# Stages in new places, layer norm outputs on GpSimd, an uneven max pass, and two head groups in one bank of sums

## The chip, the cores and the metric

The kernel runs on one core of a Trainium2 chip (trn2). The core's engines are TensorE (PE; its weight loads are PEld), VectorE (DVE), ScalarE (ACT), GpSimd (POOL) and SyncE (SP), which issues most of the DMAs. The metric is the device time of one execution in microseconds. Inputs and outputs are float32.

## The reference

One transformer block with post layer norm and no learned scale, on 16 sequences of 512 tokens and 128 features: causal attention with 16 heads of 8 features, in which the heads 0, 1 and 2 weigh one third of the keys each 1.6 times and are normalised again, and a feed-forward part of three dense layers whose weights are +1 or -1.

```python
def attention(x):                                  # (16, 512, 128)
    q, k, v = split(x @ c_attn_w + c_attn_b, 3)    # 16 heads of 8
    scores = where(causal, q @ k.T / sqrt(8), finfo.min)
    attn = softmax(scores)
    scaled = attn * mult[None, :, None, :]         # 1.6 in one region of keys, heads 0, 1, 2
    scaled = scaled / sum(scaled, -1)
    attn = where(head in (0, 1, 2), scaled, attn)
    return (attn @ v) @ c_proj_w + c_proj_b
def ffn(x):                                        # k0 (256, 512), k1 (512, 512), k2 (512, 128)
    h = relu(s0 * (concat([x, -x]) @ where(k0, 1, -1))) * 2
    h = relu(s1 * (h @ where(k1, 1, -1))) * 2
    return s2 * (h @ where(k2, 1, -1))
x = layernorm(x + attention(x))
x = layernorm(x + ffn(x))
```

## The kernel before

The program is a software pipeline over the 16 batches, written out engine by engine. `iteration(n)`, for n from -2 to 17, has G = 4 groups of four heads and STEPS = 10 steps in each; a step is written (g, t). In one iteration each engine works on several batches: the attention of batch n, the max pass of batch n + 1, q, k and the stacks of batch n + 2, the end of the attention and the first layer norm of batch n - 1, the feed-forward part of n - 1 and n - 2.

In each step TensorE computes one bank of scores for the max pass (`max_scores`, L825, into one of three banks `max_ps`) and one bank of the real, transposed scores (`scores`, L849, into one of two banks `score_ps`). VectorE takes masked row maxima from the first (`take_max`, L643), ScalarE exponentiates the second (`exp`, L516), and GpSimd sets the masked part of the result to 0 (`mask`, L423), three times in a group. Steps 0 to 3 hold the 512 keys of one head each, steps 4 to 7 pieces of 384 and 128, steps 8 and 9 two of 256. At t = 1, 3, 5, 7 TensorE adds the exponentials of the group before, times v and a column of ones (`sums`, L882), into the one bank `av_ps`, four heads at 32 rows each; at t = 9 ScalarE copies it to `avT` (`sums_out`, L523).

Queries and keys are split in three bfloat16 parts, which DMAs on SP's queue stack to 72 rows (`stack_half`, L310), so that one matmul gives the float32 score; three more rows subtract the row maximum. The maxima are split in three parts on VectorE (`split_rowmax`), transposed on TensorE (stages rowmax0 and rowmax1, L893), copied on VectorE (L683) and put into the stack by a DMA on ScalarE's queue (`rowmax_rows`, L542). Feed-forward activations are split in a high and a low part (h_hi and h_lo, L430 and L432 on GpSimd; x_hi and x_lo, L727 and L732, on VectorE).

All other work goes through two banks `bank_ps`, which the stages take in turn. The table PLACES gives for each stage the batch it works on, relative to n, the step at which TensorE fills the bank, and the step at which ScalarE or VectorE empties it; the order of the table is the order of the banks. Each engine runs its own list of instructions in order and waits on counting semaphores for the others. GpSimd's order is written out by hand in its `iteration`. So a stage that is late holds all that stands behind it on its engine. The stages: xT (transposes of the input), q, k, v, tok_0 to tok_3 (transposes of avT by 128 tokens; VectorE then normalises: reciprocal L703, product L705), attnT and proj (L967), x1T (transposes of the first layer norm's output, the sources named res), ffn0_m and ffn1_m (L909, L910), ffn2T (L924, L925) and ffn2 (its transposes).

A layer norm is: statistics (L712), aggregation (L718), minus mean and variance plus epsilon (L721, L722) on VectorE, `rstd_of` on GpSimd (a power and a product, L437 and L440), and four outputs of 128 tokens (`layernorm_out`, L534) on ScalarE.

## Time and profile before

| | |
|---|---|
| median of 3 runs | 1007.99 us (995.96, 1007.99, 1011.67) |
| the profiled execution | 994.16 us, its span 992.4 us |
| mean granted TensorE clock | 0.928 of full speed |
| PE busy | 864.0 us, 87% |
| PEld, DVE busy | 439.0 and 671.9 us |
| ACT, POOL busy | 605.0 and 502.6 us |
| first real scores, last | 73.6 us, 935.5 us |

The span is the time from the first to the last instruction of one profiled execution. The engines work side by side, so their busy times add to more than it. Between the start and the end of the program the iterations repeat with a constant period, which is what matters here.

### The profile page before, as it was taken

What the parts mean: (1) busy time and instruction counts of PE and PEld (TensorE: products, weight loads), DVE (VectorE), ACT (ScalarE), POOL (GpSimd) and SP (SyncE); (2) the same over time, 40 slices, a digit from 0 to 9 for tenths busy, and PEclk for the clock granted to TensorE, in tenths of its full rate; (3) what the DMA queues carried; (4) which work ended last, traced back from release to release, by engine and by line L of the source; (5) the groups of instructions that cost most, each with busy time, mean ns of one, the idle gap of its engine ahead of it and who ended that gap; (6) DMA issues with size and microseconds to landing.
All of it is one profiled execution on the core that took longest, in us unless ns stands there. A gap on an engine that the chain in (4) does not pass through costs nothing.

```text
span 992.4 us, 17320 instructions
## 1 busy us (share of the span) xinstructions
PE 864.0 (87%) x5824; PEld 439.0 (44%) x5824; DVE 671.9 (68%) x2784; ACT 605.0 (61%) x1106; POOL 502.6 (51%) x625
## 2 busy tenths in 40 slices
PE   2349698999999899989999998989999898999866
PEld 1114244545454454545454453545455454535343
DVE  3367578575867768595967669595857769694234
ACT  2106467566766667576757667576756767576733
POOL 1103145637564654647574664646565655547540
PEclk8558899979999997999999799999989999999887
DMA  3653635345453534455443435455443425300000
GB/s 77 68 76 60 71 51 69 45 71 56 52 63 46 74 45 66 53 71 60 53 63 45 66 45 75 49 71 59 57 54 50 70 34 73 38 23 2 23 11 11
DMA packets 66142, 53.19 MB, mean 54 GB/s; under 512 B 4518, under 2 KB 64006, under 8 KB 66054
## 3 DMA queue, kind: packets, MB, share of 16 engines
q1 hardware_dynamic: 65190, 51.30, 40.2%
q8 instruction: 47, 0.77, 0.4%
q10 hardware_dynamic: 864, 0.79, 0.3%
q14 instruction: 41, 0.34, 0.2%
HBM read 9.24 MB, written 4.19 MB: 14 GB/s over the span
## 4 chain that ended last, share of the span: by engine, by line
PE 51%; DVE 23%; POOL 9%; ACT 5%; DMA 5%; issue 4%; SPq 2%; ACTq 1%; POOLq 0%; DVEq 0%
PE av_ps L882 10%; DVE max_ps L643 10%; PE max_ps L825 10%; PE score_ps L849 8%; PE bank_ps L909 5%; POOL h_lo L432 5%; PE bank_ps L910 5%; PE bank_ps L808 4%; PE bank_ps L955 3%; DMA stack<-rowmaxT 3%; DVE stats L712 3%; POOL h_hi L430 2%; DMA stack<-parts 2%; DVE rowmax L643 2%; PE bank_ps L944 2%
## 5 line engine op out<-in xcount | busy, mean ns | idle before, releaser
L643 DVE CUSTOM_DVE_ANT_0 max_ps<-max_ps,future 128x512 f32<-128x512 f32 (+3 forms) x1024 | 480.3, 514 | 232.7 <-PE max_ps L825 229.6
L516 ACT ACTIVATE e<-score_ps 128x512 f32<-128x512 f32 x640 | 365.1, 595 | 187.7 <-PE score_ps L849 184.5
L825 PE MATMUL max_ps<-stack 72*128 72x512 bf16 (+3 forms) x1024 | 260.5, 318 | 59.9 <-DVE rowmax L643 36.1
L849 PE MATMUL score_ps<-stack 75*128 75x512 bf16 (+3 forms) x1024 | 253.8, 310 | 20.8 <-DMA stack<-rowmaxT 16.1
L423 POOL TENSOR_SCALAR_AFFINE_SELECT e<-e 128x512 f32<-128x512 f32 x256 | 160.2, 646 | 129.7 <-ACT e L516 129.7
L882 PE MATMUL av_ps<-e,vaug 128*9 128x512 f32 (+3 forms) x2048 | 194.3, 453 | 3.1 <-ACT avT L523 1.7
L825 PEld LDWEIGHTS max_ps<-stack 72*128 72x128 bf16 x1024 | 83.5, 101 | 218.0 <-DVE rowmax L643 98.3
L432 POOL TENSOR_TENSOR h_lo<-full,h_hi 128x512 fp32r<-128x512 f32 x120 | 153.4, 1278 | 10.0
L508 ACT ACTIVATE full<-bank_ps,scales 128x512 f32<-128x512 f32 x128 | 86.8, 687 | 114.3 <-PE bank_ps L910 93.1
L643 DVE DVE_READ_ACCUMULATOR2_ANT rowmax<- 128x1 f32 x1024 | 143.2, 140 | 0.0
L849 PEld LDWEIGHTS score_ps<-stack 75*128 75x128 bf16 x1024 | 90.1, 100 | 78.7 <-issue 23.8
L437 POOL TENSOR_TENSOR rstd<-var_eps,minus_half 128x4 f32<-128x4 f32 x32 | 32.5, 1015 | 151.0 <-DVE var_eps L722 151.0
L909 PE MATMUL bank_ps<-h_hi,w 128*128 128x512 f32 x256 | 106.5, 416 | 2.0 <-POOL h_lo L432 1.7
L430 POOL CAST h_hi<-full 128x512 fp32r<-128x512 f32 x120 | 73.0, 609 | 65.0 <-ACT full L508 65.0
L910 PE MATMUL bank_ps<-h_lo,w 128*128 128x512 f32 x256 | 101.1, 395 | 0.0
L406 POOL TENSOR_TENSOR qk<-qk,parts 128x1024 f32<-128x1024 f32 x15 | 31.9, 2127 | 122.5 <-ACT qk L508 122.5
L882 PEld LDWEIGHTS av_ps<-e,vaug 128*9 128x9 f32 x2048 | 31.2, 88 | 86.4 <-issue 79.7
L534 ACT ACTIVATE res<-res,shift,rstd 128x128 f32<-128x128 f32 x128 | 52.5, 483 | 15.0 <-POOL shift L440 15.0
L909 PEld LDWEIGHTS bank_ps<-h_hi,w 128*128 128x128 f32 x256 | 48.3, 189 | 20.8 <-POOL h_lo L432 6.1
L910 PEld LDWEIGHTS bank_ps<-h_lo,w 128*128 128x128 f32 x256 | 48.5, 189 | 8.7
L808 PE MATMUL bank_ps<-ident,avT 128*128 128x128 f32 x256 | 40.2, 280 | 3.3 <-ACT qk L508 2.6
L955 PE MATMUL bank_ps<-xT,wqk 128*128 128x512 f32 x64 | 38.6, 690 | 2.1 <-ACT xT L508 0.8
(83 smaller groups left out, 791.6 us busy)
## 6 DMA issues: line engine op xcount, KB each, us to landing
stack<-parts SPq DMA_DIRECT2D x288, 128.0 KB
x_in<-in_L_attn_hidden_states SPq DMA_DIRECT2D x16, 256.0 KB, 5.7
x_res<-in_L_attn_hidden_states SPq DMA_DIRECT2D x16, 256.0 KB, 11.4
out_x<-res SPq DMA_DIRECT2D x16, 256.0 KB, 10.9
stack<-rowmaxT ACTq DMA_DIRECT2D x32, 24.0 KB
e<-in_L_ffn_k SPq DMA_DIRECT2D x1, 256.0 KB, 3.5
wc<-in_L_attn_c_attn_w SPq DMA_DIRECT2D x1, 192.0 KB
e<-in_L_ffn_k SPq DMA_DIRECT2D x1, 128.0 KB, 3.3
```

What stands on the lines that cost most here:

```text
L423: last = nc.gpsimd.affine_select(out=ap, in_=ap, compare_op=ALU.is_ge, fill=0.0, base=0, pattern=[[0, 4], [1, P]], channel_multiplier=-1)
L430: nc.gpsimd.tensor_copy(h_hi[layer][:, m, :], full[:, full_slot(b, k), :]).then_inc(hi_ready, 1)
L432: nc.gpsimd.tensor_tensor(h_lo[layer][:, m, :], full[:, full_slot(b, k), :], h_hi[layer][:, m, :].bitcast(F32), ALU.subtract).then_inc(spl ...
L508: nc.scalar.activation(out_ap, bank_ps[:, u[0], :], func, **kw).then_inc(bank_free[u[0]], 1)
L516: nc.scalar.activation(e[g % 2][:, t, :], score_ps[:, t % 2, :], ACT.Exp, scale=SCALE).then_inc(exped, 1)
L643: return nc.vector.tensor_tensor_reduce(out=scored_block, in0=scored_block, in1=future[:, P * (T - 1 - qt):S], scale=1.0, scalar=NEG, op0= ...
L808: last = nc.tensor.transpose(bank[:, P * i:P * i + P], src, ident[:])
L825: return nc.tensor.matmul(out_ap[:, col:col + width], st[0:QK_ROWS, h, 0, P * qt:P * qt + P], st[0:QK_ROWS, h, 1, 0:width], start=True, st ...
L849: return nc.tensor.matmul(out_ap[:, col:col + width], st[0:ALL_ROWS, h, 1, P * kt:P * kt + P], st[0:ALL_ROWS, h, 0, P * kt:S], start=True, ...
L882: last = nc.tensor.matmul(av_ps[32 * j:32 * j + R + 1, P * kt:S], vaug[b.parity][:, kt, G * g + j, :], src, start=(order == 0), stop=(orde ...
L909: nc.tensor.matmul(bank, w, hi, start=(i == 0), stop=False)
L910: last = nc.tensor.matmul(bank, w, lo, start=False, stop=(i == len(pairs) - 1))
```

## The change

- PLACES and the tables beside it put nearly all stages to other steps. ffn1_0 and ffn1_1 now run at the end of the iteration before (group 3), ffn1_2, ffn1_3, q, k and ffn2T in group 0, tok in group 1, x1T and ffn0 from (2,6) to (3,3). xT has two buffers.
- Max pass: at the three steps of MAX_TWICE two banks of max scores are computed and taken, at the three of MAX_NONE none (`max_steps`).
- The groups of heads are now even and odd heads of a half (`head`). v has, for a pair of heads, 9 columns, 16 of zeros, 9 columns; a group takes 25 of these 34. Two groups thus add into different rows of one bank, which is copied once for both (avT has two parts, not four), and tok_0 and tok_1 transpose two blocks of 128 tokens each.
- Layer norm outputs: `normalise_tokens` on GpSimd (L472) takes the place of L534 on ScalarE. Statistics have steps of their own (LN_STATS).
- The high parts of ffn0_2 and ffn0_3 are cast on VectorE, not on GpSimd.
- SP's queue: the store of the output stands behind the load of the residual, which waits for rowmax0's bank.

```diff
 PLACES = (
-    ("ffn1_0", -2, (0, 4), (0, 4)),
+    ("xT", 2, (0, 0), (0, 0)),
+    ("q", 2, (0, 3), (0, 4)),
     ("v", 1, (0, 7), (0, 8)),
-    ("xT", 2, (0, 9), (0, 9)),
-    ("q", 2, (1, 0), (1, 1)),
-    ("tok_0", -1, (1, 2), (1, 2)),
-    ("rowmax1", 0, (1, 4), (1, 4)),
-    ("ffn2", -2, (2, 2), (2, 3)),
-    ("proj", -1, (2, 6), (2, 6)),
-    ("x1T", -1, (3, 2), (3, 2)),
+    ("ffn2", -2, (0, 9), (0, 9)),
+    ("tok_0", -1, (1, 0), (1, 0)),
+    ("rowmax1", 0, (1, 3), (1, 3)),
+    ("proj", -1, (1, 7), (1, 9)),
+    ("x1T", -1, (2, 6), (2, 6)),
+    ("ffn0_0", -1, (2, 8), (2, 8)),
+    ("ffn0_1", -1, (2, 9), (2, 9)),
-    ("ffn0_0", -1, (3, 5), (3, 5)),
-    ("ffn0_1", -1, (3, 5), (3, 5)),
+    ("ffn1_0", -1, (3, 6), (3, 7)),
...
-NEGMAX_SPLIT = (((3, 0), (3, 0), (3, 1), (3, 2)), ((1, 0), (1, 0), (1, 1), (1, 2)))
-
-NEGMAX_ROWS = ((3, 5), (1, 5))
-
-LN_VAR = ((2, 7), (2, 3))
-LN_OUT = (((3, 0), (3, 0), (3, 0), (3, 0)), ((2, 7), (2, 7), (2, 7), (2, 7)))
+FFN2_STEPS = ((0, 5), (0, 5), (0, 6), (0, 6))
+
+HIGH_STEPS = {"x1T": (2, 7), "ffn0_0": (2, 9), "ffn0_1": (3, 0), "ffn0_2": (3, 2), "ffn0_3": (3, 3),
+              "ffn1_0": (3, 7), "ffn1_1": (3, 9), "ffn1_2": (0, 1), "ffn1_3": (0, 4)}
+
+HIGH_ON_POOL = ("ffn0_0", "ffn0_1", "ffn1_0", "ffn1_1", "ffn1_2", "ffn1_3")
+
+MIDDLE_STEP = (0, 8)
+
+NEGMAX_SPLIT = (((3, 0), (3, 0), (3, 1), (3, 2)), ((0, 9), (1, 0), (1, 1), (1, 2)))
+
+NEGMAX_ROWS = ((3, 5), (1, 4))
+
+LN_STATS = ((2, 1), (3, 5))
+LN_VAR = ((2, 2), (3, 6))
+
+MAX_TWICE = ((0, 1), (0, 3), (0, 5))
+MAX_NONE = ((2, 1), (2, 2), (2, 7))
...
+        def max_steps(n, g, t):
+
+            each = [2 if (g_, t_) in MAX_TWICE else 0 if (g_, t_) in MAX_NONE else 1
+                    for g_ in range(G) for t_ in range(STEPS)]
+            first = sum(each[:STEPS * g + t])
+            for i in range(first, first + each[STEPS * g + t]):
+                quarter = i // STEPS
+                b = n + 1 if quarter else n
+                if live(b):
+                    yield b, (quarter + 3) % G, i % STEPS
+
+        def head(g, j):
+
+            return HALF * (g // 2) + 2 * j + g % 2
+
+        highs_of_dve = [w for w in HIGH_STEPS if w not in HIGH_ON_POOL]
+        HIGHS_OF_DVE = len(highs_of_dve)
...
+                if live(n + 1):
+                    wait_free(sp, use_of(n + 1, "rowmax0"))
                 if live(n):
                     if n.c > 0:
                         wait_free(sp, use_of(n + -1, "proj"))
                     sp.dma_start(x_res[:], x_tok[n.times(1)]).then_inc(xres_loaded, 16)
+                if live(n + -2):
+                    store(n + -2)
...
+            def normalise_tokens(b, i):
                 pool.wait_ge(ln_step[i], b.times(4, 3))
                 nc.gpsimd.tensor_tensor(rstd[:, i, :], var_eps[:, i, :], minus_half[:],
                                         ALU.pow).then_inc(rstd_ready[i], 1)
                 pool.wait_ge(rstd_ready[i], b.times(2, 1))
                 nc.gpsimd.tensor_tensor(shift[:, i, :], neg_mean[:, i, :], rstd[:, i, :],
                                         ALU.mult).then_inc(rstd_ready[i], 1)
+                pool.wait_ge(rstd_ready[i], b.times(2, 2))
+                x = res2 if i else res1
+                for t in range(T):
+                    ins = nc.gpsimd.tensor_scalar(x[:, t, :], x[:, t, :], rstd[:, i, t:t + 1], shift[:, i, t:t + 1],
+                                                  ALU.mult, ALU.add)
+                ins.then_inc(ln_step[i], 1)
...
+                low(1, 1)
+                low(1, 2)
+                low(1, 3)
                 masks(0, 0)
-                low(1, 0)
-                low(1, 1)
+                split_qk(0)
                 masks(0, 1)
-                low(1, 2)
+                split_qk(2)
                 masks(0, 2)
                 bias_residual()
-                split_qk(0)
                 masks(1, 0)
-                low(1, 3)
-                split_qk(2)
                 masks(1, 1)
+                layernorm_out(0)
                 masks(1, 2)
-                rstd_of_layer(1)
                 masks(2, 0)
-                rstd_of_layer(0)
-                masks(2, 1)
-                masks(2, 2)
-                masks(3, 0)
                 low(0, 0)
                 low(0, 1)
+                masks(2, 1)
+                low(0, 2)
+                masks(2, 2)
+                low(0, 3)
+                masks(3, 0)
+                layernorm_out(1)
+                low(1, 0)
                 masks(3, 1)
-                low(0, 2)
-                low(0, 3)
                 masks(3, 2)
...
+            def sums_out(b, pair):
+                act.wait_ge(summed, b.times(G, 2 * pair + 2))
+                if pair == 0 and b.c > 0:
+                    wait_full(act, use_of(b + -1, "tok_1"))
+                nc.scalar.activation(avT[:, pair, :], av_ps[:], ACT.Copy).then_inc(av_out, 1)
...
+                src = bank_ps[:, u[0], :].rearrange("p (t h o r) -> p t h o r", t=T, o=2, r=R)
+                bias = bv[:].rearrange("p (h o r) -> p h o r", o=2, r=R)
+                for o in range(2):
+                    last = nc.vector.tensor_tensor(
+                        va[:, :, :, ODD * o:ODD * o + R], src[:, :, :, o, :],
+                        bias[:, :, o, :].unsqueeze(1).broadcast_to([P, T, HALF, R]), ALU.add)
+                last.then_inc(bank_free[u[0]], 1)
...
                         src = e[g % 2][:, 8 + j // 2, 2 * P * (j % 2):2 * P * (j % 2) + 2 * P]
-                    last = nc.tensor.matmul(av_ps[32 * j:32 * j + R + 1, P * kt:S],
-                                            vaug[b.parity][:, kt, G * g + j, :], src,
-                                            start=(order == 0), stop=(order == 3))
+                    vals = vaug[b.parity][:, kt, head(g, j) // 2, (R + 1) * odd:(R + 1) * odd + ODD]
+                    last = nc.tensor.matmul(av_ps[32 * j:32 * j + ODD, P * kt:S], vals, src,
+                                            start=(order == 0 and not odd), stop=(order == 3 and odd == 1))
```

VectorE, before, from the taking of v at (0,8) to the copy of the transposed row maxima (rowmaxT) at (1,5), of one middle iteration; the left-out rows are maxima (`ISA`).

```order
L691 TENSOR_TENSOR vaug<-bank_ps,bv 128x64x8
L695 TENSOR_TENSOR vaug<-vaug,mult 128x4x3x8
L643 ISA max_ps,rowmax<-max_ps,future 128x256
...
L666 CAST rowmax_parts<-rowmax 128x4x8
L668 TENSOR_TENSOR rowmax_rest<-rowmax,rowmax_parts 128x32
...
L670 CAST rowmax_parts<-rowmax_rest 128x4x8
...
L703 RECIPROCAL recip<-bank_ps 128x16
L705 TENSOR_TENSOR attn<-bank_ps,recip 128x128
L672 TENSOR_TENSOR rowmax_parts<-rowmax_rest,rowmax_parts 128x4x8
...
L683 COPY rowmaxT<-bank_ps 24x512
```

The same stretch of VectorE in the changed kernel, up to the last part of the row maxima at (1,2):

```order
L719 TENSOR_TENSOR vaug<-bank_ps,bv 128x32x8 x2
L724 TENSOR_TENSOR vaug<-vaug,mult 128x4x2x8
...
L668 ISA max_ps,rowmax<-max_ps,future 128x512
...
L789 TENSOR_TENSOR res<-bank_ps,res 128x512
L691 CAST rowmax_parts<-rowmax 128x4x8
...
L735 RECIPROCAL recip<-bank_ps 128x32
L737 TENSOR_TENSOR attn<-bank_ps,recip 128x256
L693 TENSOR_TENSOR rowmax_rest<-rowmax,rowmax_parts 128x32
...
L695 CAST rowmax_parts<-rowmax_rest 128x4x8
...
L737 TENSOR_TENSOR attn<-bank_ps,recip 128x256
L697 TENSOR_TENSOR rowmax_parts<-rowmax_rest,rowmax_parts 128x4x8
```

The residual add of the second layer norm (L789) and both takings of attention transposes now stand between v and the last part of the row maxima.

TensorE, before, around the transposes of the first layer norm's output (sources res), from the projection on:

```order
L967 MATMUL bank_ps<-wp,attnT 128x128 x4
...
L882 MATMUL av_ps<-e,vaug 9x256 x4
...
L882 MATMUL av_ps<-e,vaug 9x512 x4
...
L808 MATMUL bank_ps<-ident,res 128x128 x4
...
L882 MATMUL av_ps<-e,vaug 9x384 x4
L893 MATMUL bank_ps<-ident_bf,rowmax_parts 24x128 x4
...
L882 MATMUL av_ps<-e,vaug 9x128 x4
L909 MATMUL bank_ps<-x_hi,w 128x512
L910 MATMUL bank_ps<-x_lo,w 128x512
```

The same place in the changed kernel; the projection now stands nine steps ahead of it:

```order
L921 MATMUL av_ps<-e,vaug 25x128 x4
L862 MATMUL max_ps<-stack 128x384
...
L886 MATMUL score_ps<-stack 128x384
...
L845 MATMUL bank_ps<-ident,res 128x128 x4
...
L921 MATMUL av_ps<-e,vaug 25x256 x4
L862 MATMUL max_ps<-stack 128x256 x2
L886 MATMUL score_ps<-stack 128x256 x2
L948 MATMUL bank_ps<-x_hi,w 128x512
L949 MATMUL bank_ps<-x_lo,w 128x512
```

The transposes moved from (3,2) to (2,6), behind the projection by nine steps and not by six, and ffn0_0 comes two steps behind them; before, it was three, with the row-max transposes between.

GpSimd, before, from the first layer norm's power on:

```order
L437 TENSOR_TENSOR rstd<-var_eps,minus_half 128x4
L440 TENSOR_TENSOR shift<-neg_mean,rstd 128x4
L423 AFFINE_SELECT e<-e 128x4x128 x4
L430 CAST h_hi<-full 128x512
L432 TENSOR_TENSOR h_lo<-full,h_hi 128x512
L430 CAST h_hi<-full 128x512
L432 TENSOR_TENSOR h_lo<-full,h_hi 128x512
L423 AFFINE_SELECT e<-e 128x4x128 x2
```

The same in the changed kernel:

```order
L464 TENSOR_TENSOR rstd<-var_eps,minus_half 128x4
L467 TENSOR_TENSOR shift<-neg_mean,rstd 128x4
L472 TENSOR_SCALAR res<-res,rstd,shift 128x128 x4
L445 AFFINE_SELECT e<-e 128x4x128 x2
L454 CAST h_hi<-full 128x512
L459 TENSOR_TENSOR h_lo<-full,h_hi 128x512
L454 CAST h_hi<-full 128x512
L459 TENSOR_TENSOR h_lo<-full,h_hi 128x512
L445 AFFINE_SELECT e<-e 128x4x128 x2
L459 TENSOR_TENSOR h_lo<-full,h_hi 128x512
L445 AFFINE_SELECT e<-e 128x4x128
```

The four outputs stand behind the power, and only one mask instruction pair lies between them and the split of ffn0_0; the masks of group 2's second set (the second `AFFINE_SELECT` x2 row) now come behind the splits of ffn0_0 and ffn0_1.

## Rows read from the trace of the kernel before

**Rows 1.** Busy time by stretch: us, then PE, PEld, DVE, ACT, POOL, clock, DMA.

```profile
376.17:433.59 57.42, 54.79 (x368) 28.53 (x364) 40.95 (x173) 38.01 (x70) 32.69 (x39) 0.91 0.45 57
433.59:488.52 54.93, 51.21 (x368) 26.43 (x364) 41.10 (x173) 37.40 (x70) 32.17 (x39) 1.00 0.49 59
```

**Rows 2.** Waits from 433.59 to 488.52: us in total, times, longest.

```profile
PEld max_ps L825 <- DVE rowmax L643: 5.7, 9, 1.1
...
PE max_ps L825 <- DVE rowmax L643: 2.2, 3, 1.4
```

**Rows 3.** Timeline from 434 to 440 us, first layer norm: start, duration, engine, line.

```profile
434.31 0.87 DVE L712 BATCH_NORM_STATS2 stats<-res 128x6 f32<-128x128 f32 x4
...
435.81 0.38 DVE L718 BATCH_NORM_AGGREGATE moments<-stats 128x2 f32<-128x6 f32 x4
...
436.10 0.38 PE L825 MATMUL max_ps<-stack 72*128 72x512 bf16 x1 [1.36 <-DVE rowmax L643]
...
436.55 1.01 POOL L437 TENSOR_TENSOR rstd<-var_eps,minus_half 128x4 f32<-128x4 f32 x1 [3.16 <-DVE var_eps L722]
...
437.87 1.65 ACT L534 ACTIVATE res<-res,shift,rstd 128x128 f32<-128x128 f32 x4 [0.54 <-POOL shift L440]
...
439.57 0.66 PE L808 MATMUL bank_ps<-ident,res 128*128 128x128 f32 x4 [0.15 <-ACT res L534]
```

**Rows 4.** Busy time by stretches of 4 us (columns as in rows 1).

```profile
376.00:380.00 4.00, 2.05 (x19) 0.94 (x12) 3.93 (x24) 3.91 (x9) 0.87 (x1) 1.00 0.72 103
...
384.00:388.00 4.00, 4.00 (x25) 1.66 (x28) 2.96 (x10) 1.37 (x4) 1.17 (x1) 0.50 0.57 80
```

**Rows 5.** Timeline from 428 to 433 us, steps (2,2) to (2,5).

```profile
428.53 0.70 DVE L643 CUSTOM_DVE_ANT_0 max_ps<-max_ps,future 128x512 f32<-128x512 f32 x1
...
429.14 0.69 DVE L756 TENSOR_TENSOR res<-bank_ps,res 128x512 f32<-128x512 f32 x1
...
429.40 0.66 PE L808 MATMUL bank_ps<-ident,attn 128*128 128x128 f32 x4
...
429.89 0.38 PE L825 MATMUL max_ps<-stack 72*128 72x384 bf16 x2
...
430.12 0.38 PE L849 MATMUL score_ps<-stack 75*128 75x384 bf16 x2
...
432.06 0.60 DVE L643 CUSTOM_DVE_ANT_0 max_ps<-max_ps,future 128x384 f32<-128x384 f32 x1
...
432.82 0.60 DVE L643 CUSTOM_DVE_ANT_0 max_ps<-max_ps,future 128x384 f32<-128x384 f32 x1
```

**Rows 6.** Groups of instructions, first the page's, then by form: busy, mean ns.

```profile
L423 POOL TENSOR_SCALAR_AFFINE_SELECT e<-e 128x512 f32<-128x512 f32 x256 | 160.2, 646 | 129.7 <-ACT e L516 129.7
L882 PE MATMUL av_ps<-e,vaug 128*9 128x512 f32 (+3 forms) x2048 | 194.3, 453 | 3.1 <-ACT avT L523 1.7
L430 POOL CAST h_hi<-full 128x512 fp32r<-128x512 f32 x120 | 73.0, 609 | 65.0 <-ACT full L508 65.0
L882 PEld LDWEIGHTS av_ps<-e,vaug 128*9 128x9 f32 x2048 | 31.2, 88 | 86.4 <-issue 79.7
L909 PEld LDWEIGHTS bank_ps<-h_hi,w 128*128 128x128 f32 x256 | 48.3, 189 | 20.8 <-POOL h_lo L432 6.1
...
L703 DVE RECIPROCAL recip<-bank_ps 128x16 f32<-128x16 f32 x64 | 16.2, 253 | 32.1 <-PE bank_ps L808 32.0
L691 DVE TENSOR_TENSOR vaug<-bank_ps,bv 128x512 f32<-128x512 f32 x16 | 11.0, 684 | 0.0
L377 POOL TENSOR_SCALAR_AFFINE_SELECT ident<-ident 128x128 f32<-128x128 f32 x1 | 0.3, 292 | 0.2 <-POOL e L373 0.2
```

**Rows 7.** Timeline from 408 to 411 us: a GpSimd and a VectorE instruction side by side.

```profile
408.90 1.29 POOL L432 TENSOR_TENSOR h_lo<-full,h_hi 128x512 fp32r<-128x512 f32 x1
...
409.50 0.81 DVE L695 TENSOR_TENSOR vaug<-vaug,mult 128x96 f32<-128x96 f32 x1
```

**Rows 8.** The chain that ended last, from 105 to 123 us.

```profile
109.72 10.41 DMA stack<-rowmaxT
```

235 lines of the change are left out of this document (113 added, 122 removed).

## The prediction, made blind

> **What bounds the kernel now.** I read first the stretches from one residual add after the projection to the next, which give the length of one period of the steady state: 54.93 us at full clock with TensorE busy 51.21, while VectorE is busy 41.1, ScalarE 37.4 and GpSimd 32.2 [rows 1]. So TensorE sets the pace, but not all of the time. The waits of that period are next: VectorE's maxima hold TensorE's weight loads for 5.7 us and its matmuls for 2.2 us [rows 2]. The two overlap and the busy share counts drains, so what TensorE loses lies between 3.7 us (54.93 - 51.21) and 7.9 us (the sum of the two waits); I take **5.4 us**, which I get when I compare steps of equal work with each other. The timeline shows where: after the projection VectorE runs the residual add, four statistics and four aggregations between its maxima, and TensorE stands for 1.36 us [rows 3]. The transposes of the layer norm output (L808, 439.57) start 3.1 us after the variance (GpSimd's pow, which waits for it, starts at 436.55).
>
> The second thing is the clock. In the period from 376.17 the granted clock was 0.91 on the mean and the period lasted 57.42 us [rows 1]. It fell to 0.50, that is from 2.4 to 1.2 GHz, right behind a stretch in which TensorE was busy 2.05 of 4 us while VectorE and ScalarE were full [rows 4]. It is the same place of the program as in rows 3. It costs 2.5 us (57.42 - 54.93) and comes in one period of three, so 0.83 us per period; the mean period is 55.76 us.
>
> **The change, part by part, for one period at full clock.**
>
> *Transposes of attention.* Two groups of heads now share the bank of sums, so four fills of four transposes become two. A fill holds TensorE for 0.49 us (429.40 to 429.89, [rows 5]): two of them less is **-1.0 us**. Two copies of avT and eight layer norm outputs leave ScalarE: the outputs alone are 8 x 0.41 us (1.65 for four, [rows 3]), but it is not what TensorE waits for, so this is worth nothing by itself. The weights of the sums grow from 9 to 25 columns. A 9-column load takes 88 ns and a 128-column one 189 ns [rows 6], so 16 columns are about 13 ns by these rows; 128 loads a period give 0 (hidden, as loads overlap matmuls) to 1.7 us. I take **+0.3**, near the hidden end, since a period's loads are busy for only 26 of its 55 us [rows 1].
>
> *First pile on VectorE.* TensorE's heavy stages (ffn1, q, k) leave the end of group 0 and the start of group 1. Count from the start of step (0,8) to the second row-max transposes at (1,3). A plain step costs TensorE 0.44 us: two matmuls that start 0.22 apart [rows 5]. The sums of a group take 3.0 us (194.3 / 64, [rows 6]), and by their columns (512 and 384 of 1280, and some overhead) about 1.9 of it lie at t = 1 and 3. TensorE's own work is 6 x 0.44 + 1.9 + 3 fills x 0.45 = 5.9 us. VectorE has five maxima (0.61 us for three of them, from 428.53 to 429.14, and 0.76 for two, from 432.06 to 432.82, [rows 5]), 3.35; the biases of v, two of 0.42 (the 684 ns of L691 less the time of 256 of its 512 columns, [rows 6]) and two small products of 0.2 to 0.8; the residual add 0.69 (429.14, [rows 5]); twice the reciprocal of 32 columns (253 ns for 16, so 0.35) with the product of 256 (as L691, 0.42), 1.6 with what passes between them; and four pieces of the row-max split, 32 columns each, at 0.2. Sum 7.8 us, and it starts 0.4 after TensorE does. That is a wait of 2.3 us at the rowmax transposes. It can be 3.3: the product L695, of only 96 columns, lasted 0.81 us when a GpSimd subtraction was running, ending 0.12 after it [rows 7], and the change puts both of GpSimd's long qk splits just there. I take **2.7**. In the kernel before, this same stretch holds ffn1_3 and the q and k matmuls, and the wait is not seen.
>
> *Layer norm 1.* VectorE's own order then gives: proj ends, residual add, one maximum, statistics 0.87, aggregation and two scalars 0.65. Then GpSimd: pow and shift 1.3 (436.55 to 437.87, [rows 3]), and four outputs of 128x128, which no row shows on GpSimd. Bounds: an affine_select of 128 columns takes 292 ns, a cast of 512 columns 609 ns [rows 6]; so 0.25 to 0.6 each. I take 0.3, near the row of equal width. From the variance to the x1T transposes this is 2.6 us (before: 3.1). TensorE has between them only (2,3) to (2,6) and is ahead by up to three maxima; the two maxima left out there make VectorE's way shorter by 1.4 us. Placed against each other the wait at x1T is 0.9 to 1.5 us, and 2.4 at the upper price: I take **1.2**. Then ScalarE's copy 0.6, VectorE's x_hi and x_lo 1.1 (estimates: passes over 512 columns, each at most the 684 ns of L691) and 0.3 of handing over make 2.0 us against 1.3 us of TensorE's work before ffn0_0: **0.85**.
>
> *GpSimd between group 2 and 3.* Its order is now both parts of ffn0_0, both parts of ffn0_1, and only then the mask of group 2's second set, on which the sums at (3,3) wait. ffn0_1 reaches GpSimd about 2.6 us after its matmuls begin (exponentials, the copy of the sums, and its own 0.7 stand before it on ScalarE); then 0.61 + 1.29 us for the parts and two masks of 0.65 [rows 6, 7]. TensorE needs 4.5 us to get to the same sums: **1.3 us** of waiting. It was not there before, where the masks stood in front.
>
> *The rest.* The cast of ffn0_2 and ffn0_3 on VectorE (below 0.69 each, as L691) lies in group 3, where I count 12.7 us of TensorE work against 11.0 of VectorE: hidden. ffn2T, v, ffn2 and ffn1 find their operands ready by my count; xT, with two buffers, and ffn1_2 at the start of an iteration lose **0.2** for a bank. The store of the output now stands behind the residual's load on SP's queue, which waits for the row-max copy at (3,4); both have a whole group 0, some 15 us of TensorE's work, before the bias add and the second residual add want them. At the start of the program four small memsets more stand before the first transpose, +0.6 us; at the end the layer norm outputs leave ScalarE, two token fills are gone, about -1 us.
>
> **Sum.** 54.93 - 5.4 (old waits) - 1.0 + 0.3 + 2.7 + 1.2 + 0.85 + 1.3 + 0.2 = 55.1 us, so at full clock the period does not change. TensorE's own work falls from 49.5 to 48.5 us and the waits grow from 5.4 to 6.3.
>
> What is left is the clock. The change cuts the long wait after the projection into pieces: none of the waits above leaves TensorE under half busy for as long as in rows 4. I expect fewer falls, and a mean period near 55.1 instead of 55.76: 14 periods x 0.65 = -9 us. Profiled execution 994.16 us, of which the span is 992.4 and 1.8 lie around it; after: **985**. The median of three runs, 1007.99, lies 13.8 us above the profiled one; by rows 1 that is five or six more falls of 2.5 us. With fewer of them in the changed kernel its median should lie close to its best run: I forecast **988 us**.
>
> A page of the Trainium skill speaks against the layer norm outputs on GpSimd: "GPSIMD Engine Reference", section "Performance versus the Vector engine", calls it the wrong choice for ordinary elementwise arithmetic, about twice as slow as VectorE. The rows show what leaves here is not VectorE's work but ScalarE's, at 0.41 us an output [rows 3]; no row has the same output on VectorE, so no row bears the factor out or refutes it. By the rule the outputs would be nearer to my upper price, and the wait at x1T nearer to 2.4 us.
>
> **Rivals.**
>
> *The piles are smaller than I placed them.* VectorE is busy only three quarters of a period [rows 1], and if the maxima of group 0, run early, let it meet group 1 with an empty queue and nothing of GpSimd blocks it, the wait of 2.7 falls to about 1 and those of 1.2 and 1.3 to about 0.5 each. Period 52.6: 14.5 x (55.76 - 52.6) = 46 us less, 948 us. For it: three maxima less where the layer norm is. Against it: VectorE's 7.8 us against TensorE's 5.9 are sums of rows, and no order of them makes them shorter. 0.24.
>
> *Falls as before.* The waits of 2.7 and then 1.2 + 0.85 lie close together, TensorE dips as low as before, and 0.83 us a period stays: 55.9, 994.16 + 2 = 996, median about 1006. The same time comes out if the 25-column loads are not hidden (+1.4), so that the shared bank gives nothing: that is the case in which the change doesn't do what it says. 0.25.
>
> *Slower: TensorE idles in one piece until x1T.* The LN outputs cost 0.6 us each on GpSimd, x1T comes 2.4 us late, ffn0_0 0.85 behind it, and the clock falls in every period, not in one of three: 55.1 + 1.2 + 2.5 = 58.8 against 55.76, so 14.5 x 3.0 = +44 us: 1038 us by the profiled execution. It decides when an output takes more than about 0.45 us. For it: 0.6 is the price of a 512-column instruction [rows 6]. 0.15. A smaller mechanism points the same way: the row-max rows of the second half leave at (1,4), one step earlier, but only some 4 us before the scores at (2,0) want them, and such a transfer took 10.41 us when others were in flight [rows 8]. The stack's transfers should be over by then.
>
> **Numbers.** My forecast has 0.36. The median of 1007.99 puts faster by over 2% below 987.8 and slower above 1028.2; about 2% is what a measurement of this kernel tells from no change, as its runs spread from 996 to 1012. Faster: the first rival whole and half of the forecast, 0.42. Slower: most of the third rival, 0.13. Same: 0.45. The range goes from 948 to 1022, with the tail of the slower case left out.
>
> **What the profile after would show.** Periods of about 55 us with VectorE near 40; a wait of 2 to 3 us of TensorE before the row-max transposes of the second half, on VectorE's split; one of about 1 us before the transposes of the layer norm output, on GpSimd's outputs at about 0.3 us; one of about 1 us before the sums of group 2 on the mask; avT's fills 32 instead of 64; fewer dips of the granted clock. I am wrong if the outputs on GpSimd take 0.45 us or more, if the period is below 53.5 or above 56.5 us at full clock, or if the clock falls in each period.

## The result, and the profile after

The changed kernel takes 1017.91 us, the median of 10 runs (1010.14 to 1035.66), beside 1003.15 us for the kernel before on the same chip: the ratio is 1.0139, with a 95% interval of 1.0095 to 1.0183. Medians are of all runs; ratios and intervals, here and below, leave out the runs that are over 1.5% slower than the fastest of the same kernel. Forecast were 988 us and a gain. It is 1.4% slower. The time lies in the range that was given (948 to 1022); the direction is wrong.

The profiled execution took 1010.14 us, with a span of 1008.4 (992.4 before). The first line of the page, busy time and share by engine:

```profile
PE 841.2 (83%) x5696; PEld 433.7 (43%) x5696; DVE 710.0 (70%) x2788; ACT 536.0 (53%) x946; POOL 542.8 (54%) x722
```

VectorE was busy 671.9 us before and should have lost some; it gained 38. The busy times by stretch (columns as in rows 1), from one batch's first score matmul to the next: one period at full clock, eleven periods together, and two stretches at the start of the second batch.

```profile
351.28:407.35 56.07, 50.06 (x357) 26.43 (x356) 43.44 (x173) 33.27 (x60) 34.76 (x46) 1.00 0.44 58
238.50:858.36 619.86, 557.17 (x3918) 293.87 (x3916) 478.34 (x1893) 366.04 (x650) 382.37 (x496) 0.99 0.44 57
126.75:144.40 17.65, 16.37 (x83) 6.68 (x84) 8.71 (x35) 8.12 (x15) 3.94 (x4) 0.72 0.54 74
144.40:158.05 13.65, 11.99 (x89) 6.03 (x89) 12.41 (x46) 7.62 (x14) 5.81 (x6) 0.87 0.01 4
```

A period at full clock takes 56.07 us, with TensorE busy 50.06. In the kernel before, the same two views give the rows below. Its periods repeat by threes, 54.31, 54.92 and 58.0 us, the last with a fall of the clock; they are not constant. Eleven take 610.99.

```profile
561.70:616.01 54.31, 50.78 (x365) 26.50 (x364) 41.09 (x173) 37.29 (x70) 31.13 (x39) 1.00 0.49 60
227.22:838.21 610.99, 573.76 (x4006) 297.11 (x4005) 451.65 (x1893) 413.16 (x760) 354.49 (x429) 0.97 0.47 58
```

So TensorE's work fell by 0.7 us as reckoned, and its idle time grew from 3.5 (54.31 - 50.78) to 6.0 us. The mean period, clock falls included, went from 55.54 (610.99 / 11) to 56.35 (619.86 / 11). What ended TensorE's waits in the period from 351.28 (waited for, us in total, times, longest; they answer to rows 2):

```profile
PE bank_ps L845 <- ACT avT L556: 1.3, 1, 1.3
PE bank_ps L931 <- DVE rowmax_parts L697: 1.2, 1, 1.2
PE bank_ps L845 <- POOL res L472: 1.1, 1, 1.1
PE av_ps L921 <- POOL e L445: 1.1, 1, 1.1
PE bank_ps L948 <- DVE x_lo L766: 0.7, 1, 0.7
PE bank_ps L948 <- ACT full L541: 0.4, 1, 0.4
```

They are, in the order of the rows: avT's transposes at (1,0), the row-max transposes at (1,3), x1T at (2,6), the sums at (3,3), ffn0_0 at (2,8), the first matmuls of ffn1 at (0,0). The prediction had a wait at all of these places but the first: it put the whole of group 1's wait on VectorE's split at (1,3) and nothing on ScalarE's copy to avT, which stands behind ScalarE's middle part of q and k. The matmuls' waits on VectorE's maxima of rows 2 are gone. The timeline ahead of the second of these waits shows what fills VectorE (start, duration, engine, line; rows 7 had this pattern once):

```profile
370.18 0.69 DVE L668 CUSTOM_DVE_ANT_0 max_ps<-max_ps,future 128x512 f32<-128x512 f32 x1
...
370.38 2.13 POOL L430 TENSOR_TENSOR parts<-qk,parts 128x1024 bf16<-128x1024 f32 x1 [1.82 <-ACT parts L615]
...
370.79 0.69 DVE L789 TENSOR_TENSOR res<-bank_ps,res 128x512 f32<-128x512 f32 x1
371.39 1.16 DVE L691 CAST rowmax_parts<-rowmax 128x32 bf16<-128x32 f32 x1
...
373.07 1.26 POOL L486 TENSOR_TENSOR x_res<-x_res,bp 128x512 f32<-128x512 f32 x1
...
373.80 0.58 DVE L693 TENSOR_TENSOR rowmax_rest<-rowmax,rowmax_parts 128x32 f32<-128x32 f32 x1
```

A cast of 32 columns takes 1.16 us and ends at 372.55, GpSimd's subtraction at 372.51. The next piece of the split ends at 374.38, GpSimd's add at 374.33. The maximum (370.18) and the residual add (370.79), each with one operand in PSUM, take their usual 0.69 beside the same subtraction. Over the whole execution L691 has a mean of 1032 ns, L693 498 and L695 465; in the kernel before the same three had 331, 387 and 185. The layer norm's chain (answers to rows 3):

```profile
386.01 1.02 POOL L464 TENSOR_TENSOR rstd<-var_eps,minus_half 128x4 f32<-128x4 f32 x1 [4.00 <-DVE var_eps L755]
...
387.42 1.74 POOL L472 TENSOR_SCALAR res<-res,rstd,shift 128x128 f32<-128x128 f32 x4
...
389.21 0.66 PE L845 MATMUL bank_ps<-ident,res 128*128 128x128 f32 x4 [1.15 <-POOL res L472]
```

From pow to the transposes it takes 3.2 us; four outputs take 1.74, 0.44 us each. The row-max transfers at the start, from the chain that ended last (answers to rows 8):

```profile
65.25 12.96 DMA stack<-rowmaxT
...
115.51 11.19 DMA stack<-rowmaxT
```

**Where 16 us of span came from.** The first score matmul starts at 78.3 us instead of 73.6 (+4.8). The first two periods take 48.4 and 55.7 us instead of 46.6 and 48.7 (+1.8, +7.0; in the second the clock is at 0.72 for 17.65 us, above). The 13 periods from there take 7.7 us more, and the end after the last batch's first score 5.3 less (95.7 for 101.0).

The 4.8 us are in part of one execution: a second profile of the kernel before (c0 below) has its first score at 75.6.

Below, "full clock" is a period in which the clock did not fall, "mean" that of the same eleven periods, and a step's time runs from its first score matmul to the next step's.

### The profile page after: what moved, and what is told of

It reads as the page before. It is cut to its first block, busy times and chain, and to the rows that moved or that the text cites. A ratio compares the mean times of both kernels' runs of the same rounds, so it can differ in the third digit from the quotient of the medians.

```text
span 1008.4 us, 16988 instructions
## 1 busy us (share of the span) xinstructions
PE 841.2 (83%) x5696; PEld 433.7 (43%) x5696; DVE 710.0 (70%) x2788; ACT 536.0 (53%) x946; POOL 542.8 (54%) x722
## 4 chain that ended last, share of the span: by engine, by line
PE 52%; DVE 19%; POOL 13%; DMA 5%; ACT 4%; issue 4%; SPq 2%; ACTq 0%; POOLq 0%; DVEq 0%
PE av_ps L921 9%; PE max_ps L862 9%; PE score_ps L886 7%; PE bank_ps L948 7%; DVE max_ps L668 7%; PE bank_ps L949 6%; POOL h_lo L459 4%; PE bank_ps L994 3%; POOL res L472 3%; PE bank_ps L845 3%; ACT full L541 3%; DMA stack<-rowmaxT 2%; DMA stack<-parts 2%; POOL h_hi L454 2%; POOL e L445 2%
## 5 line engine op out<-in xcount | busy, mean ns | idle before, releaser
L862 PE MATMUL max_ps<-stack 72*128 72x512 bf16 (+3 forms) x1024 | 249.6, 315 | 26.5 <-DMA stack<-parts 19.4
L886 PE MATMUL score_ps<-stack 75*128 75x512 bf16 (+3 forms) x1024 | 249.3, 306 | 22.8 <-DMA stack<-rowmaxT 18.7
L921 PE MATMUL av_ps<-e,vaug 128*25 128x512 f32 (+3 forms) x2048 | 194.2, 452 | 18.1 <-POOL e L445 17.8
L862 PEld LDWEIGHTS max_ps<-stack 72*128 72x128 bf16 x1024 | 80.0, 100 | 175.1 <-issue 87.9
L886 PEld LDWEIGHTS score_ps<-stack 75*128 75x128 bf16 x1024 | 94.6, 100 | 91.0 <-ACT e L549 25.3
L454 POOL CAST h_hi<-full 128x512 fp32r<-128x512 f32 x90 | 54.9, 610 | 76.5 <-ACT full L541 76.5
L921 PEld LDWEIGHTS av_ps<-e,vaug 128*25 128x25 f32 x2048 | 37.7, 102 | 89.6 <-issue 55.8
L948 PEld LDWEIGHTS bank_ps<-h_hi,w 128*128 128x128 f32 x256 | 48.8, 190 | 22.5 <-ACT full L541 8.3
L472 POOL TENSOR_SCALAR res<-res,rstd,shift 128x128 f32<-128x128 f32 x128 | 56.3, 455 | 3.3
L949 PEld LDWEIGHTS bank_ps<-h_lo,w 128*128 128x128 f32 x256 | 48.8, 191 | 9.0
L430 POOL TENSOR_TENSOR parts<-qk,parts 128x1024 bf16<-128x1024 f32 x15 | 31.9, 2128 | 24.7 <-ACT parts L615 24.7
## 6 DMA issues: line engine op xcount, KB each, us to landing
x_in<-in_L_attn_hidden_states SPq DMA_DIRECT2D x16, 256.0 KB, 16.3
```

Source lines behind the costliest of these rows:

```text
L454: nc.gpsimd.tensor_copy(hi, whole).then_inc(hi_by_pool, 1)
L472: ins = nc.gpsimd.tensor_scalar(x[:, t, :], x[:, t, :], rstd[:, i, t:t + 1], shift[:, i, t:t + 1], ALU.mult, ALU.add)
L862: return nc.tensor.matmul(out_ap[:, col:col + width], st[0:QK_ROWS, h, 0, P * qt:P * qt + P], st[0:QK_ROWS, h, 1, 0:width], start=True, st ...
L886: return nc.tensor.matmul(out_ap[:, col:col + width], st[0:ALL_ROWS, h, 1, P * kt:P * kt + P], st[0:ALL_ROWS, h, 0, P * kt:S], start=True, ...
L921: last = nc.tensor.matmul(av_ps[32 * j:32 * j + ODD, P * kt:S], vals, src, start=(order == 0 and not odd), stop=(order == 3 and odd == 1))
L948: nc.tensor.matmul(bank, w, hi, start=(i == 0), stop=False)
```

## Experiments

### The waits of the changed kernel, one by one

**e1: masks of (2,1) ahead of the low part of ffn0_1** on GpSimd.

```diff
-                low(0, 1)
                 masks(2, 1)
+                low(0, 1)
```

> The changed kernel, with one line moved in GpSimd's list: the masks of group 2's second set (2,1) stand before the split of ffn0_1, not behind it. In the changed kernel TensorE stands about 1.0 us per period before the sums at step (3,3) (2.72 us for a step whose work is 1.7). Theory A (each wait is its own and returns when its cause goes): the period falls from 56.08 to about 55.1 us, the run by about 14 us. Theory B (VectorE is the bound from group 1 to group 3; a wait removed comes back at the next place): the wait of (3,3) goes to the row-max transposes behind it, since VectorE's split and its two casts lie there, and the period stays within 0.3 us of 56.08.

1016.42 us, ratio 1.0124 (1.0027 to 1.0221). The wait for the mask is gone, but step (3,3) only falls from 2.72 to 2.46 us; in its place the row-max transposes there wait 0.7 us for L697 (1.9 us in two waits where there was 1.2 in one). Full clock 55.82, 0.25 less. Theory B.

**e2: ScalarE's middle part of q and k one step later.**

```diff
-MIDDLE_STEP = (0, 8)
+MIDDLE_STEP = (0, 9)
```

> The changed kernel with ScalarE's cast of the middle part of q and k one step later (0,9), so that it no longer stands before the copy of the sums (avT) on which the token transposes at (1,0) wait (1.5 us of waiting there, 1.2 us more at the row-max transposes of (1,3)). If ScalarE's copy is the cause of both, 1 us of the 2.7 goes and the period falls to about 55.1. If VectorE's pile between (0,8) and (1,2) is, as the prediction had it, the wait only moves from (1,0) to (1,3), and the period stays within 0.3 us of 56.08.

1080.17 us in its one run. Step (1,0) falls from 2.39 to 1.44 us, as avT's copy now stands ahead of the middle part, but (1,2) and (1,3) grow from 0.88 and 2.91 to 1.85 and 4.29, and the clock falls in every period, from within (1,3) on: mean 61.4. Neither reading had that. The trace shows what fills (1,3):

```profile
453.87 2.14 POOL L430 TENSOR_TENSOR parts<-qk,parts 128x1024 bf16<-128x1024 f32 x1 [2.80 <-ACT parts L615]
...
453.91 2.14 DVE L691 CAST rowmax_parts<-rowmax 128x32 bf16<-128x32 f32 x1
```

The middle part reaches GpSimd later, so its subtraction now begins together with the cast, and the cast takes the whole 2.14 us.

**e3: the max pass even again** (both tables empty).

```diff
-MAX_TWICE = ((0, 1), (0, 3), (0, 5))
-MAX_NONE = ((2, 1), (2, 2), (2, 7))
+MAX_TWICE = ()
+MAX_NONE = ()
```

> The changed kernel with the max pass even again, one bank in each step (nothing taken twice, nothing left out). Theory A: VectorE then has three maxima more (2.1 us) between (1,9) and (2,7), where the layer norm chain holds TensorE; the wait at (2,6) grows by about 1.5 us and that at (2,8) by 0.7, while group 0 is TensorE's anyway: the period rises to 57.5 to 58.3 us, the run by 20 to 30 us. Rival: the maxima fit behind the transposes, since GpSimd's outputs take longer than VectorE's part, and the period stays within 0.4 us of 56.08.

1056.71 us (four runs from 1036.21 to 1079.61), ratio 1.0372 (1.0284 to 1.046); mean 58.07, with a fall in each period. TensorE waits 1.9 us for x1T and 1.9 for maxima. The uneven pass is worth 1.7 us a period in the changed kernel, falls included. Theory A by its period.

**e4: the second row-max split from (0,7) on**, `((0, 7), (0, 7), (0, 8), (0, 8))` for `((0, 9), (1, 0), (1, 1), (1, 2))`.

> The changed kernel with the four pieces of the second half's row-max split at (0,7), (0,7), (0,8), (0,8) on VectorE instead of (0,9) to (1,2). The uneven max pass has finished that half by (0,6), and VectorE is idle there. Prediction's reading (the row-max transposes at (1,3) wait for VectorE's whole pile): the wait of 1.2 us at (1,3) goes, VectorE's way to the layer norm becomes about 0.8 us shorter, and the period falls by 0.8 to 1.5 us, to 54.6 to 55.3. Rival: VectorE's work in group 1 is the bound whatever its order, TensorE then waits for free banks of the max pass, and the period falls by 0.3 us or less.

1021.19 us, 1.0223 (1.0149 to 1.0298); full clock 56.3. The wait for L697 at (1,3) is gone (2.91 to 1.52 us), but (1,2), (1,4) and (1,6) grow from 0.88, 0.44 and 0.44 to 1.15, 0.69 and 1.46, where TensorE waits for the maxima themselves and for an exponential. That looks like the rival, a VectorE full of its own work, but the trace shows the collision in a new place:

```profile
592.22 2.12 POOL L430 TENSOR_TENSOR parts<-qk,parts 128x1024 bf16<-128x1024 f32 x1 [1.82 <-ACT parts L615]
...
592.23 2.16 DVE L697 TENSOR_TENSOR rowmax_parts<-rowmax_rest,rowmax_parts 128x32 bf16<-128x32 f32 x1
```

The last piece of the split, 0.18 us when free, begins with GpSimd's subtraction and takes 2.16, and the maxima behind it are late.

**e8: the casts of ffn0_2 and ffn0_3 back on GpSimd** (added to HIGH_ON_POOL).

> The changed kernel with the casts of ffn0_2 and ffn0_3 back on GpSimd. Theory A (a VectorE row is late only where its own work is long): VectorE loses 0.84 us a period around (2, 6) to (2, 9) and the period falls by up to 0.5 us, to 1008 to 1016. Theory B (GpSimd's long instructions hold VectorE up): the two casts lie on GpSimd between the layer norm outputs and block VectorE there; the waits at (2, 8) and (3, 3) grow by 0.5 to 1.5 us each, 1020 to 1045.

1028.18 us, 1.0249 (1.018 to 1.0318). Full clock 56.40, and from the eighth period on 58.0 with a fall in each:

```profile
563.70:621.70 58.00, 53.16 (x356) 27.46 (x356) 40.84 (x171) 33.54 (x59) 35.80 (x47) 0.94 0.42 56
```

VectorE is relieved of 2.6 us and the period is longer. The predicted growth at (2,8) and (3,3) did not come; (3,6) did, by 0.33. Theory B's sign, not its place.

**e5: layer norm outputs back on ScalarE**, at (2,5) and (3,8).

> The changed kernel with the layer norm outputs back on ScalarE, at (2, 5) and (3, 8), where GpSimd makes them now; all else is the change's. Theory A (GpSimd's outputs at 0.455 us each, which also hold VectorE up, are what the changed kernel lost): the wait at (2, 6), 2.03 us, becomes 1.3 to 1.6 and the ones at (2, 8) and (3, 3) shrink by 0.3 each, so a period of 54.8 to 55.5 and 990 to 1005 us. Theory D (the new places of the stages lose by themselves: two waits in group 1 and those at (0, 0) and (3, 3), whoever makes the outputs): 55.8 to 57 us a period, 1008 to 1030 us, since ScalarE's outputs stand ahead of exponentials.

1026.77 us, 1.0234 (1.0144 to 1.0323); full clock 56.30, mean 57.95. x1T waits 1.4 us for ScalarE instead of 1.1 for GpSimd. Theory D: the outputs on GpSimd are not what was lost.

### The part that blocks

**e7: GpSimd's two subtractions of q and k over 8 of 512 columns** (that part of the split is left out).

```diff
...
-  nc.gpsimd.tensor_tensor(pt[:, 2:6:3, :], qk[:], pt[:, 1:5:3, :], ALU.subtract)
+  nc.gpsimd.tensor_tensor(pt[:, 2:6:3, 0:8], qk[:, :, 0:8], pt[:, 1:5:3, 0:8], ALU.subtract)
```

> The changed kernel with the two subtractions of GpSimd's q and k split made over 8 of their 512 columns, which leaves out that part of the split (the rest of the parts is not what the reference needs). The second of them, 1.28 us, runs beside the cast of VectorE's row-max split that takes 1.03 us instead of 0.17. Theory B (GpSimd's long instructions hold VectorE up, and the piles of group 1 come from that): the waits at (1, 0) and (1, 3), 2.39 and 2.91 us with their work, lose 0.8 to 1.5 us together, and the period falls to 54.6 to 55.3. Theory A (the pile is VectorE's own work and the copy of the averages behind ScalarE's middle part): the two steps lose under 0.3 us, the period stays over 55.7.

997.97 us, 0.9944 (0.9902 to 0.9987). Step (1,0) stays at 2.39; (1,3) falls from 2.91 to 1.57 us. The first cast, now with no long subtraction beside it (that one has shrunk to 0.22 us; the expectation's 1.28 us for it in the changed kernel should read 2.13):

```profile
364.40 0.17 DVE L692 CAST rowmax_parts<-rowmax 128x32 bf16<-128x32 f32 x1
```

Full clock 54.78, 1.3 us less, all of it at one step.

**a2: all of the work, the subtraction a step earlier**, ahead of masks(0, 1), with MIDDLE_STEP at (0, 7).

> The changed kernel with ScalarE's middle part of q and k one step earlier, at (0, 7), and GpSimd's second subtraction ahead of masks(0, 1): it then runs beside VectorE at (0, 8) and (0, 9), not beside the row-max split of group 1. Theory B (the collision is what costs): (1, 3), 2.91 us, falls to 1.6 to 2.0 and the period to 54.8 to 55.3 at full clock, 995 to 1005 us, nearly as e7_qk_small. Theory J (the subtraction holds VectorE wherever it stands, or the masks come late now): the time comes back at (0, 9), (1, 0) or (1, 3), the period stays over 55.8 us.

1088.93 us, 1.0844 (1.0774 to 1.0914), mean 62.2. Its timeline in group 1:

```profile
385.08 2.14 POOL L430 TENSOR_TENSOR parts<-qk,parts 128x1024 bf16<-128x1024 f32 x1 [1.52 <-ACT parts L615]
...
388.95 1.28 POOL L486 TENSOR_TENSOR x_res<-x_res,bp 128x512 f32<-128x512 f32 x1
```

```profile
386.16 1.15 DVE L724 TENSOR_TENSOR vaug<-vaug,mult 128x64 f32<-128x64 f32 x1
...
388.99 1.27 DVE L691 CAST rowmax_parts<-rowmax 128x32 bf16<-128x32 f32 x1
```

The subtraction now blocks the vaug product (1.15 us for 0.23) and the residual add behind it blocks the cast. The clock then falls in each period and costs more than the pile. Theory J. **a3: e1's order on top of it.**

> a2_middle_earlier and e1_mask_first together. If their effects add, 0.26 us less at (3, 3) and 54.5 to 55.0 us a period, 990 to 1000 us; if VectorE's row is full in group 3 anyway, as e1_mask_first showed in part, within 0.2 us of a2_middle_earlier.

1080.29 us, 1.0764 (1.0686 to 1.0842), mean 0.5 us a period under a2 (61.7 for 62.2). Step (3,3) falls from 2.73 to 2.46 us, as by e1 alone, so the two effects add, which was the first case; the times forecast for it fell with a2's.

**a4: both GpSimd instructions later**, behind masks(0, 2) and masks(1, 0), where GpSimd was idle.

```diff
                 masks(0, 1)
-                split_qk(2)
                 masks(0, 2)
-                bias_residual()
                 masks(1, 0)
+                split_qk(2)
+                bias_residual()
```

> The changed kernel with all of its work; GpSimd's second subtraction (2.13 us) and the add of the bias to the residual (1.26 us) stand behind masks(1, 0) instead of around masks(0, 2), so they run in steps (1, 3) to (1, 6), where GpSimd is idle for 4.62 us and VectorE has only PSUM maxima. SP stacks these parts in group 2 only, so nothing waits for them sooner. Theory B (their blocking of VectorE's row-max split is what the piles of group 1 cost beyond VectorE's own work): (1, 3) falls from 2.91 to 1.5 to 1.7 us as in e7_qk_small and the period to 54.7 to 55.1, 995 to 1003 us, 1.5% under the changed kernel. Theory J (the collision moves on, as in a2_middle_earlier): the last step of the split (L697) or the vaug products are blocked instead, 55.8 us or more, 1012 us or more.

996.23 us, median of 10; 0.995 (0.991 to 0.9989) of the kernel before, where the changed kernel has 1.0139. One period, and its group 1:

```profile
569.38:624.11 54.73, 49.92 (x357) 26.45 (x356) 42.09 (x173) 33.22 (x60) 34.74 (x46) 1.00 0.47 60
```

```profile
367.79 0.17 DVE L691 CAST rowmax_parts<-rowmax 128x32 bf16<-128x32 f32 x1
...
371.62 0.18 DVE L697 TENSOR_TENSOR rowmax_parts<-rowmax_rest,rowmax_parts 128x32 bf16<-128x32 f32 x1
```

```profile
372.52 2.13 POOL L430 TENSOR_TENSOR parts<-qk,parts 128x1024 bf16<-128x1024 f32 x1
374.62 1.26 POOL L486 TENSOR_TENSOR x_res<-x_res,bp 128x512 f32<-128x512 f32 x1
```

TensorE's and GpSimd's busy times are those of the changed kernel, VectorE's is 1.35 us less, and the period is 1.34 us shorter: (1,3) is 1.58 us, as in e7. Theory B. This settles the cause at (1,3) with all of the work done.

### The parts on the kernel before

**b1: the uneven max pass alone**, in the kernel before, with MAX_TWICE = ((0, 4), (0, 6), (0, 9)) and MAX_NONE = ((2, 7), (2, 8), (3, 0)).

> The kernel before with one part of the change alone: its tables, its GpSimd order, its banks and its ScalarE layer norm outputs stay, and only the max pass is made uneven (two score matmuls of it in steps (0, 4), (0, 6) and (0, 9), none in (2, 7), (2, 8) and (3, 0)). Theory A (each wait has its own cause, as the prediction reckoned): the waits of the max pass at (2, 7), (2, 8) and (3, 0), part of the 5.4 us that the prediction took off, go here too, and without the five waits that the rest of the change added the period at full clock falls from 54.93 to 51.5 to 53, so about 940 to 970 us. Theory B (VectorE's stretch from (2, 5) to (3, 3) is the bound, and a wait removed reappears at its next product): the period stays within 0.8 us of 54.93, the whole within 1% of before.

993.26 us, 0.988 (0.9819 to 0.9942); mean 54.67 for 55.54.

```profile
731.28:785.73 54.45, 50.96 (x366) 26.74 (x365) 41.23 (x173) 37.39 (x70) 32.18 (x40) 1.00 0.45 60
```

At full clock it takes 54.41 and 54.45 us, between the 54.31 and 54.92 of before: the waits for maxima became waits for ScalarE (1.4 us for an exponential, 0.8 for layer norm outputs). It gains since the long falls, one in three periods, are gone. Theory B by its period, with a gain that neither theory had.

**s1: the shared bank alone**, with the old tables, order and ScalarE outputs (all banks and weights of the change).

> The changed kernel's banks with the tables of the kernel before: two groups of heads share the bank of the sums, with 25-column weights and one copy of it in two groups instead of each, two token fills less, x transposed into two buffers; the max pass is even, layer norm outputs are on ScalarE and GpSimd's order is the one of before. Theory A (the prediction's terms): -1.0 for the fills and +0.3 for the wider weight loads, so a period of 54.2 at full clock, 988 to 1003 us. Theory C (the shared bank holds the sums of the next group up, since its copy and its reciprocals come once in two groups and the wait at (0, 0) costs 0.8 rather than 0.2): 55 us or more, 1003 to 1015.

1010.56 us, 1.0072 (1.003 to 1.0114); full clock 54.40.

```profile
576.70:631.10 54.40, 49.95 (x358) 26.02 (x357) 41.25 (x171) 36.33 (x68) 31.05 (x39) 1.00 0.49 60
```

TensorE is busy 0.8 us less than at 561.70 of the kernel before and the period is the same: the two fills stood in waits, which are now longer (step (1,7) grew from 1.09 to 2.04 us as (1,5) and (1,6) shrank by 0.9). The clock was lower (0.95 over the eleven periods, 0.97 before), mean 56.35. Neither theory's reason.

**s2: bank and uneven pass.**

> The kernel of s1_bank_alone with the uneven max pass as well, so all of the change but the new places of the stages and GpSimd's layer norm outputs. Theory A: the gain of b1_uneven and that of s1_bank_alone add, 51 to 52.5 us a period and 930 to 960 us; what made the whole change slower is then its moved tables and GpSimd's outputs. Theory B: no better than the kernel before, 54 to 56 us a period.

994.03 us, 0.9894 (0.9833 to 0.9955), mean 54.65, full clock 54.1 to 54.8: as b1 (54.67 on the mean). The bank adds nothing. What is left at step (2,9), 1.76 us for 0.38 of matmuls:

```profile
390.52 1.63 ACT L559 ACTIVATE res<-res,shift,rstd 128x128 f32<-128x128 f32 x4
...
392.69 0.39 PE L890 MATMUL score_ps<-stack 75*128 75x512 bf16 x1 [1.37 <-ACT e L541]
```

**s3: s2 with the second layer norm's outputs on GpSimd.**

> The kernel of s2_bank_uneven (old places, shared bank, uneven max pass) with the second layer norm's outputs on GpSimd, right behind its shift, instead of ScalarE at (2, 7). In s2_bank_uneven TensorE waits at (2, 9), 1.76 us for 0.38 us of matmuls, while ScalarE is busy without a gap, four outputs among it. Theory H (ScalarE's outputs make that wait): (2, 9) falls to 0.5 to 1.0 us and the period to 53.0 to 53.5 at full clock, 975 to 985 us. Theory I (VectorE's statistics of the first layer norm and its transposes set the stretch from (2, 6) to (3, 2), so ScalarE's relief comes back at (3, 1) or (3, 2), or GpSimd's outputs block VectorE's statistics): 54 to 55 us, 990 to 1005.

996.17 us, 0.9926 (0.9884 to 0.9969); full clock 54.3 to 54.8. Step (2,9) fell to 0.63 us and (3,2) grew by as much, from 1.81 to 2.93:

```profile
388.61 0.66 PE L855 MATMUL bank_ps<-ident,res 128*128 128x128 f32 x4 [1.83 <-ACT res L567]
```

Theory I. **s4: both layer norms' outputs on GpSimd.**

> The same with both layer norms' outputs on GpSimd, so that s2_bank_uneven and the whole change now differ from it in one part each. If GpSimd's outputs (4 of 0.455 us where ScalarE's stand between exponentials) are good in the old places too: 53 to 54 us a period, below 990 us, and the new places alone cost the change 2 us or more. If they are what costs: 55.5 to 57 us, 1005 to 1030 us, since the transposes of (3, 2) wait for outputs that block VectorE's maxima.

1011.44 us, 1.0023 (0.9975 to 1.007). Its periods at full clock are 54.2 to 54.7 us in five cases and 55.4 in two, but from the twelfth on each has a fall (58.0). So GpSimd's outputs cost nothing at full clock in the old places; by time the second case came (1005 to 1030), and what the time lost against s3 lies in the falls.

**s5: s3 with x1T's transposes a step later**, at (3, 3).

> s3_pool_ln1 with the transposes of x1 and the split of them one step later, (3, 3) and (3, 4). In s3_pool_ln1 the 1.1 us that (2, 9) gained came back at (3, 2), 2.93 us for 1.10 us of matmuls, where those transposes wait for ScalarE's outputs of the first layer norm. Theory K (that chain alone makes the wait, and 1.5 us of cover are worth as much): (3, 2) falls to about 1.2 us, (3, 5), where ffn0_0 waits for the split, grows by 0.5 to 1.0, the period falls by 0.7 to 1.2 us to 53.1 to 53.7 and the whole to 975 to 985 us. Theory L (the wait only moves to (3, 3) and (3, 5)): within 0.3 us of s3_pool_ln1, 988 to 1000 us.

1062.39 us, 1.0592 (1.049 to 1.0693), mean 60.1. Step (3,2) is still 2.70 us:

```profile
413.34 0.39 PE L896 MATMUL score_ps<-stack 75*128 75x512 bf16 x1 [2.10 <-ACT e L549]
```

ScalarE's four outputs stand ahead of the exponential, and the scores wait for that. Both theories fell.

### The start

**c0: the kernel before, profiled again.**

> The kernel before, unchanged, once more with a profile: its first profiled execution was the fastest of 13 runs (995.96 us, where their median is 1003.6), and the first score of its third batch came at 168.9 us, where seven other kernels of this study, three with its own order at the start, show 178 to 183 us. Theory F (the start is a matter of one execution, its transfers and clock falls): this profile shows 174 to 182 us there and a span of 998 to 1005 us, with the periods at full clock as before (54.3 to 54.9). Theory G (the start before was truly shorter, and each change to the order spoils it): 167 to 171 us again.

995.92 us, span 994.0. The third batch's first score comes at 169.8 us (168.9 the first time), and the periods repeat. Theory G: its short start is no accident of one execution.

**e6: the first half of batch 1 stacked only when batch 0's row-max rows have landed.**

```diff
+                if b.c == 1:
+                    sp.wait_ge(rowmax_in[0], 16)
```

> The changed kernel with one wait more ahead of its loop: SP stacks the first half of batch 1 only once the row maxima of batch 0's first half have landed in the stack. Theory C (the 16 stack transfers of batch 1 in flight make the row-max transfer 12.96 us instead of 10.2 and so delay the first score): that transfer falls to 3 to 6 us, the first score comes at 69 to 74 us instead of 78.3, and the whole gains 3 to 9 us. Theory E (the transfer takes its time by itself, or the first half of batch 1 is late in turn): it stays over 9 us or the first period grows by what the start gains, and the whole stays within 3 us.

1017.87 us, 1.0122 (1.0002 to 1.0243), as the changed kernel. The transfer takes 2.80 us instead of 12.96, the first score comes at 66.7 us, 11.6 earlier, and the first period takes 68.7 us instead of 48.4:

```profile
63.77 2.80 DMA stack<-rowmaxT
...
72.03 17.22 DMA stack<-parts
...
100.63 10.03 DMA stack<-rowmaxT
```

The first period grew by 20.3 us where the start had gained 11.6, and the third batch's first score comes at 191.0 us (182.4 in the changed kernel), yet the medians are equal. Theory E, by its second half: the stack's transfers, held back, are late in turn.

## Why the prediction was wrong

**What bounds the kernel, and the clock.** Right that TensorE sets the pace and that the clock fell one period in three. The base was 0.3 us high: 54.93 was the longer of the two periods at full clock (mean 54.6). In the changed kernel the falls became short (clock 0.99 on the mean over eleven periods, 0.97 before), as forecast, but the run did not gain by it.

**The step that failed: "Sum ... so at full clock the period does not change".** It came to 56.07, not 55.1. (TensorE's own work in that sum should read 48.8 us, 49.5 - 1.0 + 0.3, not 48.5; and the first rival's terms give 51.9, not 52.6. Neither changes the forecast.) Term by term, by step times:

- *The waits that were added*: 2.7 forecast for group 1, all at (1,3) and on VectorE, measured 2.7, but 1.5 of it at (1,0) on ScalarE's copy to avT, which the prediction did not have, and 1.2 at (1,3): the sum agrees by luck; x1T 1.2, measured 1.15; ffn0_0 0.85, measured 0.92; masks 1.3, measured 1.0, and e1 shows VectorE's split 0.7 us behind them; the bank at (0,0) **0.2, measured 0.8** (the wait in the rows is 0.4 of it); the copy of the second averages at (1,9), 0 forecast, 0.28. Together 6.85 for 6.25.
- *The 5.4 us that were taken off.* b1 and s3 show how such a wait is to be read: with VectorE's maxima out of the way ScalarE's exponentials were late in the same place (1.4 us), and with those out of the way its layer norm outputs (1.8 us; in s4, with these on GpSimd, 2.0 for GpSimd), each time with nearly the same period at full clock. A wait was read as one cause's loss, where three engines were late together.
- *-1.0 for two fills*: s1 measured 0 at full clock. The fills stood before a wait.

The +0.3 for wider weight loads has no run of its own; a load of 25 columns takes 102 ns on the mean, 14 more than one of 9, as reckoned. The added waits account for 0.6 of the 1.0 us; the other 0.4 (0.7 from the mean base of 54.6) lies in the terms taken off, and no run splits it further.

**The cause that matters is inside a term whose size agreed by luck.** The pile at (1,3) was reckoned as 2.3 us of VectorE's own work, with the blocking as an extra of up to 1.0 ("It can be 3.3 ... the change puts both of GpSimd's long qk splits just there"), of which 0.4 was taken. The runs show the reverse: without the blocking TensorE does not wait for VectorE at (1,3) at all (a4, e7), so the whole 1.3 us there is the blocking. Whether VectorE's own pile would show once ScalarE's wait at (1,0) is gone too stays open: no run takes both away, as e2 made the collision longer. a4 takes the blocking out by the places of two GpSimd instructions: 1.34 us a period, and 1.9% of the time by the two ratios to the kernel before (0.995 / 1.0139). At full clock a4 (54.73) and s4 (54.70), which has the old places and, but for two casts on VectorE and the order on SP's queue, the same parts, are equal: the new places gain nothing, and all that they cost there is this collision. That they should gain was never in the sum; "VectorE near 40" was in the list of what the profile would show, and at 43.4 it named the fault.

The Trainium skill has this: "SBUF — State Buffer", section "SBUF: two separate sides", says that GpSimd and VectorE share one pair of ports, held by one of them for its whole instruction, for VectorE's two-port modes and, against a GpSimd instruction that reads SBUF, for its operations with two SBUF inputs. The rows agree in every case shown: the blocked instruction ends 0.03 to 0.09 us after GpSimd's.

**The clock term, -9 us.** Measured +0.28 us a period of short falls in the eleven periods (56.35 - 56.07), against 0.9 before (55.54 - 54.6). So 0.65 us a period was won, where all of the falls' cost was forecast to go, and the longer period took it back.

**Start and end.** +0.6 was forecast for the start, a term that no run shows by itself, and +13.6 came (4.8 + 1.8 + 7.0); -1 for the end and -5.3 came, as the stages moved ahead leave less behind the last batch (95 to 98 us in every kernel with the new places, 100 to 102 in every one with the old). Of the start, c0 shows that it is real; in e6 the first row-max transfer was fast and nothing was gained in all. b1, which only moves maxima, has the third batch at 180.0 us too, also with low clock behind the second row-max wait. What decides whether the clock comes back there stays open.

**The rivals.** The slower one was to decide at 0.45 us an output. They took 0.44 from start to start (0.455 as the page's mean), just at that point, but the wait was 1.1 and not 2.4, and the clock did not fall in each period: the sign came by another way. In all, the forecast missed 1.25 us in each of the 13 periods behind the start (56.35 for 55.1; 1.0 of it the period at full clock, 0.3 the short falls), 16.3 us, and 8.7 us at the ends (8.3 for -0.4): the 25 us between 985 and 1010. The rule that the prediction named, from the Trainium skill's "GPSIMD Engine Reference", section "Performance versus the Vector engine", compares GpSimd with VectorE (1.96 times the time, for an add of two tensors). No run here has the outputs on VectorE, so none tests it. Against ScalarE it is no guide: an output took 0.44 us on GpSimd and 0.41 on ScalarE, and e5, with the outputs on ScalarE, was slower.

## What to carry over

When an engine's small instruction is several times its usual length, look for what its neighbour was running and compare the ends; here moving two GpSimd instructions behind two groups of masks was worth 1.9%, more than any part of the change by itself. When a piece is moved away from such a collision, look where the long instruction lands next (e2, e4, a2), before the engine's own work is blamed. A wait that is taken away pays only up to the next engine's, so test a part alone (b1, 0.988) before moving everything. The best versions here are b1, s2 and s3, 0.7 to 1.2% under the kernel before.

## What the runs showed of the hardware

- VectorE's casts and sums from SBUF, where a GpSimd instruction ran first, ended 0.03 to 0.09 us after it: 32 columns took 2.14 us for 0.17 (e2), 2.16 for 0.18 (e4). Its maxima and the residual add, with one operand in PSUM, kept their 0.69 beside the same subtraction.
- In a2 the steps (1,0), (1,2) and (1,3) together took 1.9 us more than in the changed kernel (8.09 for 6.18, the clock at 0.77 in the last of them), and the period, with a fall of the clock in each, 5.9 more (62.2 for 56.35); e8 and s4 changed from few falls to one a period in mid-run without any change in the work.
- A row-max transfer took 12.96 us while the stack's transfers kept the DMA engines 0.57 busy, and 2.80 with these held back (0.03).
